# Expert stages whose 128-row pieces stay open across chunks of batches, shared batches ahead of the sorted ones, and a memset between indirect transfers

## What is computed

```python
def ffn(x, sg_w, su_w, sd_w, router_w, routing_bias, wg, wu, wd):   # x: normalised rows
    shared = silu(xt @ sg_w.T) * (xt @ su_w.T) @ sd_w.T
    probs = sigmoid(xt @ router_w.T + routing_bias)          # 8 experts
    topk_p, topk_idx = top_k(probs, 2)
    topk_p = topk_p / sum(topk_p)
    h = silu(xt @ wg[e].T) * (xt @ wu[e].T)                  # for each expert e
    y = h @ wd[e].T
    return shared + sum over the two chosen e of topk_p[e] * y[e]
x = x + attn_a(norm(x)); x = x + ffn(norm(x)); x = x + attn_b(norm(x)); x = x + ffn(norm(x))
```

## Time and profile before

| | us |
|---|---|
| median of 3 runs | 1383.76 (1382.67 to 1384.84) |
| profiled execution, its own time | 1393.95 |
| its span, first to last instruction | 1392.2 |
| TensorE matmul busy | 957.8 (69%) |
| VectorE busy | 657.1 (47%) |
| ScalarE busy | 607.2 (44%) |
| GpSimd busy | 457.9 (33%) |
| mean granted TensorE clock | 0.831 |

### The profile page before, as it was taken

How to read it: one execution, slowest core, us unless ns; L and a number is a source line. 1 busy time by engine, 2 the same in 40 slices (tenths; PEclk the granted TensorE clock), 3 DMA queues, 4 the chain that set the end, 5 groups by cost and what they waited for, 6 DMA issues and landing times.

```text
span 1392.2 us, 19740 instructions
## 1 busy us (share of the span) xinstructions
PE 957.8 (69%) x6976; PEld 569.3 (41%) x6976; DVE 657.1 (47%) x1314; ACT 607.2 (44%) x876; POOL 457.9 (33%) x527
## 2 busy tenths in 40 slices
PE   4776388528588766878787878786756078799241
PEld 3665256426355323333333333333333056566120
DVE  4787234202132345786777777775363033222022
ACT  1231063103145564777686877766422034254020
POOL 1113410640610343554433333342117600401734
PEclk9787589769889677999898999996587599999665
DMA  9400210121224344344443434311001211122222
GB/s 304 144 1 19 62 32 16 48 68 37 72 69 141 127 151 151 130 150 140 142 142 123 142 125 156 116 44 55 31 1 46 67 31 31 61 74 83 60 66 81
DMA packets 110557, 123.29 MB, mean 89 GB/s; under 512 B 9472, under 2 KB 72832, under 8 KB 110336
## 3 DMA queue, kind: packets, MB, share of 16 engines
q1 hardware_dynamic: 81664, 95.01, 20.9%
q0 software_dynamic: 8192, 16.79, 4.1%
q10 hardware_dynamic: 20608, 10.23, 2.5%
HBM read 60.52 MB, written 61.47 MB: 88 GB/s over the span
## 4 chain that ended last, share of the span: by engine, by line
PE 40%; DVE 16%; another core or an unknown queue 15%; issue 10%; DMA 9%; ACT 5%; SPq 4%; POOL 1%; DVEq 0%; POOLq 0%; ACTq 0%
PE psum L758 8%; DVE ring_b L1675 7%; PE psum L1470 5%; PE psum L1422 5%; PE psum L781 4%; DMA stacks<-stack_qr 4%; PE psum L724 2%; PE psum L771 2%; SPq L1820 2%; PE psum L735 2%; PE psum L1487 2%; DMA stacks<-stack_ky 2%; SPq L1815 2%; PE psum L743 1%
## 5 line engine op out<-in xcount | busy, mean ns | idle before, releaser
L1675 DVE TENSOR_SCALAR ring_b<-psum 128x1024 int32<-128x1024 int32 x160 | 195.7, 1223 | 129.0 <-PE psum L1422 128.8
L1549 ACT ACTIVATE ring_a<-psum 128x1024 f32<-128x1024 f32 x160 | 163.5, 1026 | 140.9 <-PE psum L1422 139.3
L1422 PE MATMUL psum<-stacks 32*128 32x128 f32 (+3 forms) x1024 | 107.1, 399 | 129.8 <-DVE ring_b L1675 97.2
L1555 ACT ACTIVATE ring_b<-ring_b 128x1024 f32<-128x1024 f32 x160 | 168.6, 1055 | 44.3 <-DVE ring_b L1675 44.3
L960 POOL DMA_INDIRECT r_rows<-y_sorted,rows_of x128 | 128.3, 1002 | 180.7 <-DMA y_sorted<-y_out 133.9
L758 PE MATMUL psum<-w_expert,ring_a 128*128 x312 | 160.8, 640 | 32.5 <-ACT ring_a L878 27.7
L950 POOL DMA_INDIRECT x_sorted<-r_rows,rows_of x128 | 124.1, 970 | 157.8 <-DVE rows_of L1170 120.5
L1781 POOL TENSOR_SCALAR_AFFINE_SELECT ring_b<-ring_b 128x512 f32<-128x512 f32 (+1 forms) x112 | 81.6, 741 | 284.5 <-ACT ring_b L1555 284.5
L1204 DVE TENSOR_TENSOR ring_b<-psum,ring_b 128x512 f32<-128x512 f32 x80 | 54.2, 677 | 223.9 <-ACT ring_b L863 184.9
L1422 PEld LDWEIGHTS psum<-stacks 32*128 32x128 f32 x1024 | 62.9, 201 | 225.0 <-ACT ring_a L1549 84.8
L1667 DVE TENSOR_SCALAR ring_a<-ring_a 128x1024 f32<-128x1024 f32 x160 | 122.7, 770 | 34.4 <-ACT ring_a L1549 34.4
(11 more groups left out here) (175 smaller groups left out, 1291.5 us busy)
## 6 DMA issues: line engine op xcount, KB each, us to landing
ring_a<-x_sorted SPq DMA_DIRECT2D x36, 256.0 KB
y_sorted<-y_out ACTq DMA_DIRECT2D x36, 256.0 KB
stack_q<-parts SPq DMA_DIRECT2D x32, 256.0 KB
stack_ky<-parts SPq DMA_DIRECT2D x32, 256.0 KB
stacks<-stack_q SPq DMA_DIRECT2D x32, 256.0 KB
stacks<-stack_ky SPq DMA_DIRECT2D x32, 256.0 KB
stack_k<-parts SPq DMA_DIRECT2D x32, 256.0 KB
stacks<-stack_k SPq DMA_DIRECT2D x32, 256.0 KB
```

Of the source, the lines that this page charges most:

```text
L1422: mm = nc.tensor.matmul(bank(2 * pair + j % 2)[:, column:column + width], keys[rows, s, kb * 128:(kb + 1) * 128], queries[rows, s, q0:q0 + ...
L1549: nc.scalar.activation(exps[:, n % RING, 2 * u:2 * u + 2, :], psum[:, first:first + 2, :], ACT.Exp, scale=SCALE).then_inc(self.exp, 1)
L1555: nc.scalar.activation(part, part, ACT.Ln, bias=1.0).then_inc(self.ln, 1)
L1675: nc.vector.tensor_scalar(ring[:, m % RING, HEADS_B[u][0]:HEADS_B[u][1] + 1, :].bitcast(I32), psum[:, first:first + 2, :].bitcast(I32), 0x ...
```

## The change

1. The two groups become chunks of batches, `CHUNKS_1, CHUNKS_2 = (4, 4), (3, 3, 2)`, with one sorted array for all. A slot (now "page") that an expert has begun in one chunk is filled further by the next; only pages that are surely full after chunk 0 (`quads_soon`: 6 quads in the first stage, 4 in the second) are worked on before all chunks are sent. There are 71 pages for each stage instead of 78 slots, 36 pairs instead of 40.
2. The chain of VectorE is longer: 49, 42 and 38 links for a first, middle and last chunk, against 26 and 5 for a group.
3. In the first stage all eight shared batches come before the first pair. Routing of chunk 0 comes one step later in the first attention. GpSimd's queue holds there: 20 sends, rstd of the first late batch, 12 sends, rstd of the others. The fetched block is still of batches 1 to 3, the attention's steps are counted from pair 27 of 36.
4. In the second stage chunks 0 and 1 are routed within the last steps of the second attention and sent three transfers a step, then without steps; rstd of batch 8 stands behind them in GpSimd's queue. Batches 1 to 6 are fetched before the last two.
5. Behind each send, and each fetch of batches 1 to 4 that is done in a block, GpSimd does a memset of 128 x 384 and waits for it (`pause`).

The diff, cut to its core:

```diff
-SIZES_1, SIZES_2 = (3, 5), (6, 2)
+CHUNKS_1, CHUNKS_2 = (4, 4), (3, 3, 2)
...
-            ffn_1.send(p, 0)
+            ffn_1.send(p, 0, 0, 20)
+            ffn_1.pool_rstd(p, ffn_1.first_late)
+            ffn_1.send(p, 0, 20)
+
+        pause_room, paused, pauses = sb("pause_room", [128, 384]), sem("paused"), [0]
+
+        def pause(p):
+            pauses[0] += 1
+            nc.gpsimd.memset(pause_room[:], 0.0).then_inc(paused, 1)
+            p.wait_ge(paused, pauses[0])
...
+                self.all_pairs, self.all_quads = (PAGES + 1) // 2, (PAGES + 3) // 4
+                self.early = B - chunks[-1]
+                self.first_late = self.early + 1
+                self.quads_soon = (2 * chunks[0] * TT - ROUTED + 1) // 4
+                self.first_in_rest = 7 if led else 4
+                self.offset = 0 if led else len(shared_first)
+                self.scored = B - self.first_late + 3
+                self.lead_from = self.all_pairs - 9
...
             def tensor(self, pe):
                 if self.led:
                     self.previous.wait_done(pe)
+                else:
+                    for n, b in enumerate(self.shared_first):
+                        self.shared_gate_up(pe, b, 0)
+                        if n == self.scored + 1:
+                            self.tensor_ranks(pe, len(self.chunks) - 1)
+                        if n > 0:
+                            self.shared_down(pe, b - 1)
+                        self.shared_gate_up(pe, b, 1)
+                        self.late_tensor(pe, n)
+                    self.shared_down(pe, self.shared_first[-1])
                 self.quad_turn(pe, 0)
...
-            def send_tiles(self, p, g, first, last):
+            def send(self, p, c, first=0, last=None):
...
+                        in_=x_rows[:, (at + t) // TT, t % TT, :], in_offset=None).then_inc(self.sent_soon if c == 0 else self.sent, 16)
+                    pause(p)
...
                         self.fetch_tile(p, b, n, t)
+                        if b <= 4:
+                            pause(p)
...
+                if k == 15:
+                    self.pool_rstd(p, self.first_late)
+                if 11 <= k < 19:
+                    self.send(p, 0, 3 * (k - 11), 3 * (k - 10))
+                if 19 <= k:
+                    self.send(p, 1, 3 * (k - 19), 3 * (k - 18))
 
             def pool(self, p):
                 if self.led:
-                    self.send_tiles(p, 0, 3 * (11 - self.sizes[0]), 2 * self.tiles(0))
-                for b in range(self.first_late, B + 1):
+                    self.send(p, 1, 3 * (2 * DUS + 3 - 19))
+                for b in range(self.first_late + 1, B + 1):
                     self.pool_rstd(p, b)
-                self.send(p, 1)
-                for b in range(1, self.first_late):
+                self.send(p, len(self.chunks) - 1)
+                for b in range(1, self.first_in_rest):
                     self.fetch(p, b)
...
                 for n in range(self.all_quads):
-                    g, first, many = self.quad_slots(n)
-                    if first == 0:
-                        sp.wait_ge(self.sent, 16 * 2 * TT * (self.sizes[0], B)[g])
+                    first, many = self.quad_slots(n)
+                    if n == 0:
+                        sp.wait_ge(self.sent_soon, 16 * 2 * self.tiles(0))
+                    if n == self.quads_soon:
+                        sp.wait_ge(self.sent, 16 * 2 * (TT * B - self.tiles(0)))
...
             def vector(self, v):
                 late = self.first_late
-                if self.led:
-                    self.vector_stats(v, late)
+                if not self.led:
+                    for n, b in enumerate(self.shared_first):
+                        if late + n <= B:
+                            self.vector_bias(v, late + n)
+                        self.shared_hidden(v, b, 0)
+                        if n > 0:
+                            self.add_shared(v, b - 1)
+                        self.shared_hidden(v, b, 1)
+                        self.late_logits(v, n)
+                        self.late_vector(v, n)
+                    self.add_shared(v, self.shared_first[-1])
                 for j in range(self.all_pairs):
...
-        ffn_1 = Experts("f1", AttentionDone(), SIZES_1, shared_first=(),
-                        shared_after={7: (1,), 9: (2, 3), 11: (4, 5), 13: (6, 7), 15: (8,)}, adds_after={22: (1,), 25: (2,), 27: (3,)})
+        ffn_1 = Experts("f1", AttentionDone(), CHUNKS_1, shared_first=tuple(range(1, B + 1)),
+                        shared_after={}, adds_after={26: (1,), 29: (2,), 33: (3,)})
...
-        ffn_2 = Experts("f2", log_attn, SIZES_2, shared_first=(1, 2, 3),
-                        shared_after={1: (4,), 3: (5,), 5: (6,), 7: (7,), 9: (8,)}, adds_after={33: (1,), 36: (2,), 38: (3,)},
-                        led=True)
+        ffn_2 = Experts("f2", log_attn, CHUNKS_2, shared_first=(1, 2, 3),
+                        shared_after={1: (4,), 3: (5,), 5: (6,), 29: (7,), 33: (8,)},
+                        adds_after={23: (1,), 27: (2,), 30: (3,), 34: (4,)}, led=True)
```

More of the change, by code:

```diff
@@ L545, in orders @@
                 down = [("shared", b) for b in self.shared_first]
-                turns = [("quad", 0)]
+                late_turn = lambda n: [("turn", self.batch_turned(n))] if self.first_late <= self.batch_turned(n) <= B else []
+                turns = [user for n in range(self.offset) for user in late_turn(n)] + [("quad", 0)]
                 for j in range(self.all_pairs):
@@ L575, in is_early, with tiles, own, kind @@
+            def tiles(self, c):
+                return TT * self.chunks[c]
+            def own(self, c):
+                return slice((self.first_of(c) - 1) * TT, self.last_of(c) * TT)
+            def kind(self, c):
+                return "first" if c == 0 else "last" if c == len(self.chunks) - 1 else "middle"
+            def chain_at(self, c, n):
+                return sum(LINKS[self.kind(k)] for k in range(c)) + n
             def is_early(self, b):
-                return b <= self.sizes[0]
+                return b <= self.early
@@ L578, in turn_room @@
             def turn_room(self, b):
                 return bank((0 if self.led else 4) if self.is_early(b) else 6)
-            def route_bank(self, g):
-                return 7 if g == 1 else 1 if self.led else 4
-            def one_by_one(self, g):
-                return g == 0 and not self.led
-            def logit_count(self, g):
-                return sum(self.sizes[0] if self.one_by_one(k) else 1 for k in range(g + 1))
-            def logit_room_of(self, g, first, last):
-                return psum[:, self.route_bank(g), first * ROUTED:last * ROUTED]
@@ L614, in pair_slots @@
             def pair_slots(self, j):
-                g = 0 if j < self.pairs[0] else 1
-                j -= g * self.pairs[0]
-                return g, [i for i in (2 * j, 2 * j + 1) if i < self.slots[g]]
+                return [i for i in (2 * j, 2 * j + 1) if i < PAGES]
             def quad_slots(self, n):
-                g = 0 if n < self.quads[0] else 1
-                first = 4 * (n - g * self.quads[0])
-                return g, first, min(4, self.slots[g] - first)
+                return 4 * n, min(4, PAGES - 4 * n)
             def last_pair_item(self, n):
@@ L767, in pair_turn @@
                 pe.wait_ge(self.h_copied, j)
[L768 removed]
+                for m in range(len(self.pair_slots(j))):
                     for c in range(IC):
@@ L1012, in pool @@
                 else:
-                    for b in range(self.first_late, B + 1):
+                    for b in range(self.first_in_rest, B + 1):
                         self.fetch(p, b)
@@ L1118, in vector_second @@
                 v.wait_ge(self.chain, at + 9)
-                tt(score, left, self.spread(g, best[2]), ALU.is_equal).then_inc(self.chain, 1)
+                tt(score, left, self.spread(c, best[2]), ALU.is_equal).then_inc(self.chain, 1)
                 v.wait_ge(self.chain, at + 10)
@@ L1801, in pool @@
             def pool(self, p):
-                for n in range(STEPS_A + DUS + LAG + 2):
+                for n in range(STEPS_A + 2 * DUS + 3):
                     self.pool_step(p, n)
```

614 lines of the change are left out of this document (359 added, 255 removed).

## The result

| | before | after |
|---|---|---|
| median, us | 1384.30 (4 runs, 1382.67 to 1388.09) | 1368.87 (4 runs, 1364.88 to 1369.74) |
| ratio to before | | 0.9882, 95% interval 0.9843 to 0.9921 |
| profiled execution, its own time | 1393.95 | 1369.74 |
| its span | 1392.2 | 1368.0 |
| GpSimd busy | 457.9 | 538.3 |

The change made the kernel faster by 1.2%, 15 us; the forecast was 45 us.

What follows compares the result with a forecast made beforehand. Late TensorE signals in transfer bursts were taken to cost some 170 us; with pauses, GpSimd's queue binds. Gains of 13.4 us (first stage) and 32 (second) took 45.4 off: 1348.6 profiled, 1338.4 median, range 1295 to 1398.

Steps and rivals of the forecast that it cites:

- forecast (a): Whole kernel: pauses work and GpSimd's queue is the bound; 1338 us, own range 1310 to 1365, chance 0.55.
- the cadence: Paused sends and fetches: one indirect transfer start to the next, taken as 1.70 us, between 1.53 and 1.76.
- quad 6: First stage: TensorE does pairs 0 to 9 (250 to 284 us), then stands at quad 6's turn until 310.
- The attention with its drain: Second attention, with two chains beside its drain: end at 1064 us instead of 1062.12, bounds 0 and +15.
- Six shared batches at 6.3 give 241: First stage: from 203.6 us, six shared batches at 6.3 us each end at 241.
- The lead is one pair shorter, 45.6: Between rstd and start of the second attention: 49.1 us shrinks by one pair to 45.6, start at 444.3.
- on the path as long as the pairs are: Expert stages: 36 pairs instead of 40 take 13 us less TensorE work in each stage, 26 in both.
- I take the same microseconds off: Median without profile: the 45.4 us gained in the profiled execution come off 1383.76 too, giving 1338.4.
- The tail, 30.0 us: End of kernel: from the last store to the end stays 30.0 us, with 16 unpaused fetches in it.
- the 10 us of late signals ahead of it: Unpaused fetches of batches 5 and 6, from about 1301 us: late signals cost up to 20 us, 10 taken.
- That is some 170 us: Kernel before: late TensorE signals in bursts of sends and fetches cost some 170 of 1392.2 us.
- rival (b): Whole kernel: the memset does not free the signals; 98 us more, 1436 us, slower; chance 0.20.

Runs made afterwards that it cites:

- e4: The changed kernel with GpSimd's queue reordered (rstd of late batches and the clearing of values earlier), no work added, chip 10: 1315.3 us, ratio 0.9463 to before.
- e6: e4 with three memsets of 128 x 8, each with a wait, in place of each one of 128 x 384, chip 12: 1307.6 us.
- e8: e4 with shared batches moved behind the pairs that don't wait for the send, chip 12: 1276.3 us, ratio 0.9862 to before.
- e9: The kernel before, unchanged, run again on chip 12: 1290.9 us.
- e10: The changed kernel without pauses, on chip 12: 1302.0 us, ratio 1.0096 to before.
- e1: The changed kernel without pauses, on chip 10: 1398.2 us, ratio 1.0080 to before.
- e15: e8 without pauses, on chip 4: 1357.5 us, ratio 0.9758 to before.
- e2: The kernel before with only the pauses added (each send, each block fetch of batches 1 to 4), chip 10: 1358.7 us, ratio 0.9795.
- e14: e6 repeated on chip 4: 1311.8 us, ratio 0.9440 to before.
- e5: The changed kernel as it is, run again on chip 12: 1368.4 us, ratio 1.0578 to before.
- e13: e12 repeated on chip 4: 1268.0 us, ratio 0.9130 to before.
- e12: e8 with pause memsets of 192 columns in place of 384, chip 12: 1260.3 us, ratio 0.9754 to before.
- e3: The changed kernel with pause memsets of 128 x 8 in place of 128 x 384, waits kept, chip 10: 1379.2 us, ratio 0.9918 to before.

## Why the prediction was right or wrong

Right: the direction (0.71 for faster), the mechanism of forecast (a), and most of its places. Pauses free the signals; the cadence is 1.67 (taken 1.70); rstd of batch 5 ended at 179.06 (182), that of batch 6 at 200.27 (203.6); TensorE stood 24.2 us at quad 6 (26 by the forecast's own times), 23.5 us at pair 1 of the second stage (30), and 32.9 at pair 6. The attention with its drain grew by 2.8 us (1.9), which is less than it varies: its length lies between 603 and 612 us in before, after, e4, e6, e8 and e9. From the end of the attention to the end of the kernel it was 1392.2 - 1062.12 = 330.1 us, and is 1368.0 - 1071.15 (the second stage's first L740) = 296.9: 33.2 us gained, forecast 1392.2 - 1062.12 - (1360 - 1064) = 34.1. That this agrees so well is partly luck, as step 4 shows.

Wrong by 30 us of 45. The steps that failed are the first stage's time for six shared batches (1) and the shorter lead of the second attention (2); the reference for the median (3) did the rest. In turn:

1. **"Six shared batches at 6.3 give 241", first stage.** Busy time by stretch, 201 to 264 us: first TensorE's matmuls (busy, count), then those of L740 alone with their weight loads; behind them the granted clock, the share of the transfers and GB/s:

```profile
201.00:264.00 63.00, 48.95 (x249) 0.79 0.06 17
...
201.00:264.00 63.00, 22.72 (x72) 14.68 (x72) 0.79 0.06 17
```

   The gate and up products of six batches (72 of L740) and the down products of seven took 63 us, 9 to 10.5 us a batch. The price of 6.3 was from two batches in a row between pairs, with nothing between, at a mean granted clock of 0.99 (205 to 247 us of before). Here stand also the scores, turns and ranks of batches 5 to 8 (4.86, 2.36 and 3.99 us of TensorE), and five waits of 1.4 to 6.0 us for VectorE (adding the bias, its chain, products), at a mean granted clock of 0.79: behind the waits of 14.52, 2.69 and 6.04 us TensorE was granted its lower level, 1.2 GHz, for some microseconds (a clock of 0.50 from 199 to 207, from 219 to 222 and from 250 to 258 us, of 0.99 and more from 207 to 217; six of L740 took 2.90 us at 201.22 and 1.65 at 207.10). I had counted the late batches' steps in the second stage, not in the first. The second send began at 265.93 in place of 251, and all that hangs on it moved with it: quad 6 at 323.1 (310), fetches from 371.3 (353), the attention's rstd at 415.35 (398.7).

2. **"The lead is one pair shorter, 45.6".** From the end of that rstd to the attention's first scores it was 49.1 us before and is 463.97 - 415.35 = 48.6; in e4 50.1, in e9 49.1, in e10 48.3. It is longer only in e1 and e15 (52.9 and 61.8), which have late signals. It is a chain of transfers and small steps that doesn't shorten with the pairs: with 36 pairs TensorE is done sooner and waits 18.4 us for `stack_ky`, with 40 it waited 9.0 (9.5 in e9, 9.0 in e2). So the first stage's 13 us of TensorE work, "on the path as long as the pairs are", was off the path there, and I had shortened the lead for it once more. Steps 1 and 2 make the first stage lose 6.25 us (463.97 against 457.72) in place of gaining 13.4: 19.7 us, all of the miss in the profiled execution (45.4 against 24.2) but 1.5.

3. **"I take the same microseconds off" for the median.** The profiled executions differ by 24.2 us, the medians by 15.4. The profiled execution of before stands 9.7 us above its median, that of after 0.9, so 8.8 us of what was read from the trace were not in the median to be won. Nineteen executions of the kernel before on chip 10 lie between 1380.9 and 1398.6, ten on chip 12, where no signal is late, between 1288.2 and 1296.6. That the lateness itself scatters would fit this, but isn't shown. A forecast should have been set against the median of before.

4. **The tail, 30.0 us, and the 10 us of late signals ahead of it.** From the last store (1334.84) to the end it is 33.2 us. GpSimd's timeline, where the fetches of batches 4 to 8 begin, and their last:

```profile
1305.41 0.95 POOL L1010 DMA_INDIRECT r_rows<-y_sorted,rows_of  x1 [6.81 <-DMA y_sorted<-y_out]
...
1358.25 0.94 POOL L1010 DMA_INDIRECT r_rows<-y_sorted,rows_of  x1 [0.30 <-issue]
```

   40 fetches run with no gap over 1.1 us between them, so the last store no longer ends a wait: GpSimd is still fetching when it lands. The error of 3 us was paid for by signals that came earlier than feared: I had taken 10 us of lateness, 20 at most, on the unpaused fetches of batches 5 and 6, and TensorE waited 2.87 and 2.07 us there. Two wrong terms cancelled.

5. **"That is some 170 us".** This didn't enter the sum, but it made the pauses look worth more than they can be. On chip 12, where no signal is late, the kernel before takes only 90 to 99 us less than on the first chip and chip 10. Part of what was read as lateness was time that TensorE stands for sent rows in any case: of the 49 us put down to it behind the attention's end, 27.4 us remain on chip 12 (e9).

The deeper error is one the trace of before could not show. I took its late signals for what every such chip does; they were there on three chips (first, 10 and 4) and not on another (12). The rival (b), slower because the pauses buy nothing, had 0.20 with the reason that 1.7 us might be too fast. On chip 12 it is what happens, for another reason: there is nothing to buy. The prediction's reading of the Trainium skill ("SBUF — State Buffer", section "Who interferes with whom"), that a memset would hold the shared port as a transfer does and free nothing, left out the section's conditions: VectorE contends with GpSimd only in its 2-port modes, or with two inputs in SBUF against a GpSimd instruction that reads SBUF. A memset only writes, and the additions and products that were late have one input in PSUM. The runs agree that the memset's hold on a port is not what matters: e14 and e4 differ by a factor of 16 in columns written and come out alike (1311.8 and 1315.3).

## What to carry to other kernels

A pause buys engine time and costs queue time. Before putting one in, ask what is queued behind it: here late signals cost 96 us (1390 against 1294 for the kernel before, 1398 against 1302 for the changed one without pauses), the longer queue took back 66 (e5, e10), and moving six rstd and one memset ahead in it, which adds no work, was worth 53 us across chips (e4) and 61 on one chip (e6 against e5, there with three short memsets for each pause). Shorter work on the engine that looks busiest is worth nothing ahead of a serial chain whose length was 48 to 50 us in the five executions named above. And a stall that a trace puts down to "issue" should be looked for on a second chip before a kernel is tuned around it.

## What the runs showed of the hardware

- In a burst of indirect transfers of 128 rows, one each 1.27 us, signals from TensorE to VectorE and ScalarE came 3 to 26 us late on three chips (before on the first, e1 on chip 10, e15 on chip 4). On a fourth, chip 12, they came at once with the same programs and the same pace of transfers (e9, e10), and the kernel before took the same time there in two separate sets of runs (1293.9 and 1291.6). Kernels with enough pause took the same time on both kinds within 0.7% (after: 1368.9 and 1368.4; e14 and e6: 1311.8 and 1307.6; e13 and e12: 1268.0 and 1260.3).
- On chips with late signals 1.36 us a transfer was too fast (e3, chip 10, one memset of 8 columns) and 1.52 slow enough (e13, chip 4, one of 192), as was 1.68 with one long memset or three short ones (e4, e14). No chip saw both 1.36 and 1.52. What differs between the chips, whether it stays with a chip, and what holds the signals, no run here shows. It wasn't tried whether one long gap after several transfers does as well as a gap after each.
